# Cross-attention in blocks of three score units, keys and values made by halves of 16 heads, on one Trainium2 core

## The chip, the cores and the metric

The kernel runs on one core of a Trainium2 chip. The metric is the device time of one execution in microseconds (us); the time of before is the median of three runs. The engines are TensorE (PE in the rows; PEld is its weight load), VectorE (DVE), ScalarE (ACT), GpSimd (POOL) and SyncE (SP), whose queue here issues nearly every DMA.

## What is computed

A decoder layer on x of shape 4 x 512 x 512 with a context of 4 x 1601 x 512: a gated recurrence (HGRN), a cross-attention, a self-attention and a mixture of experts, each with a post layer norm. The change touches the cross-attention alone:

```python
q = x @ Wq.T                       # 4 x 512 x 512, 32 heads of 16
k_raw = context @ Wk.T             # 4 x 1601 x 512
v_raw = context @ Wv.T
# heads of 16 columns; keys and values stand interleaved in kv
q = _rmsnorm(q); k = _rmsnorm(k)
scores = jnp.einsum('bhnd,bhmd->bhnm', q, k) * 16 ** (-0.5)
attn = jax.nn.softmax(scores, axis=-1)
out = jnp.einsum('bhnm,bhmd->bhnd', attn, v)
```

## The kernel before, in words

Everything is float32. Products of inputs and weights are made in three terms (high x high, high x low, low x high) of fp32r parts by `product3`; it is L120 of the profile.

**Units of work.** The context of a batch is 13 tiles of 128 rows (CT, the last partly filled). A *quad* is 4 heads (HG); a batch has 8 quads (NQ). A *tile* of the softmax is one quad with one context tile: 4 batches x 8 quads x 13 = 416 tiles. A tile has two *score units*, each two matmuls of 64 rows side by side into two PSUM banks (`scores`, L859), and for each unit ScalarE makes one exponential of 128x1024 (L705). After both, four matmuls, which run as eight, sum the products with the values into one bank, `o_bank` (L876, the *sum* of the tile). Scores turn through three pairs of banks, the probabilities through two buffers.

**Pieces.** What feeds the softmax is cut into pieces. X transposes a tile of x (L830) and VectorE splits it (L738, L740). Q, K and V are projections of 12 matmuls each, in two halves of 6. K and V use all 512 columns, 32 heads. VectorE copies the results (L744 `raw`, L755 `vt`), makes the mean squares (L713 to L719), GpSimd the power of -1/2 (L683 `c_rr`), and VectorE scales (L725 `c_kn`). T transposes the scaled keys or queries (L843) and VectorE splits them (L770, L772). SP stores keys, queries and values into the DRAM tensors `kd`, `qd`, `vd` (L598, L611, L602) and loads them as quads `kq`, `qq`, `vq` (L635, L622, L626), double-buffered. O transposes the sums of a finished quad (L847), and VectorE adds them to X (L778 to L784). All pieces of the softmax share one PSUM bank, bank 7.

**Order.** `Timeline` writes the order out. A prologue makes all pieces of batch 0 (4 X, 4 Q, 13 K, 13 V, 17 T), stores them, and then both of its first quads are loaded. Then comes one loop over the 416 tiles, where TensorE has for each tile: two score units ahead, the sum of the tile, then at most one piece or half product, `line.after[lt]`. The pieces of batch b+1 lie under the softmax of batch b, so the softmax of batch 3 has O pieces alone. In the prologue ScalarE makes the high parts of the context tiles (L699) and VectorE the low ones (L731); later GpSimd makes both (L671, L673), behind its power for the job.

The inner part of TensorE's loop before:

```python
for u in (2 * lt + 3, 2 * lt + 4):
    if u < UNITS:
        scores(u)
pe.wait_ge(s_ex, 2 * lt + 2)
...
for piece in line.after[lt]:
    put(piece)
```

Of the kernel before, what the change touches and what calls it, by code (L numbers as in the profile page):

```python
# [19 lines left out]
P = 128  # L20
# [11 lines left out]
HG = 4  # L32
# [426 lines left out]
class Piece:  # L459


    def __init__(self, kind, job, half, last, item):
        self.kind, self.job, self.half, self.last, self.item = kind, job, half, last, item


class Timeline:


    JOBS = TT + CT
    LTS = (XH // HG) * CT  # L470

    def __init__(self):
        self.items, self.index = 0, {}
        self.prologue = [p for p in self.steps(0)]
        self.prologue_items = self.items
        total = B * self.LTS
        self.after = [[] for _ in range(total + 4)]
        for b in range(B):
            todo = self.plan(b + 1) if b + 1 < B else []
            for lt in range(b * self.LTS, (b + 1) * self.LTS):  # L480
                if lt > CT and lt % CT == 1:
                    self.after[lt] = [self.piece("O", lt // CT - 1, 0, 1)]
                elif todo:
                    kind, job, half, halves = todo[0]
                    if half + 1 == halves and lt % CT == CT - 1:
                        continue
                    self.after[lt] = [self.piece(*todo.pop(0))]
            assert not todo
        self.after[total + 1] = [self.piece("O", total // CT - 1, 0, 1)]

    def plan(self, b):
        at = lambda j: b * self.JOBS + j
        turn = lambda j: [("T", at(j), 0, 1)]
        project = lambda kind, j: [(kind, at(j), 0, 2), (kind, at(j), 1, 2)]
        out = [("X", at(0), 0, 1)]
        for j in range(TT):
            if j + 1 < TT:
                out.append(("X", at(j + 1), 0, 1))
            out += project("Q", j)
            if j >= 2:  # L500
                out += turn(j - 2)
        for j in range(TT, self.JOBS):
            out += project("K", j) + turn(j - 2) + project("V", j)
        return out + turn(self.JOBS - 2) + turn(self.JOBS - 1)

    def steps(self, b):
        return [self.piece(*s) for s in self.plan(b)]
# [8 lines left out]
def cross_attention(nc, X, ident, d):  # L516
# [16 lines left out]
    with ExitStack() as stack:  # L533
# [51 lines left out]
        def _(sp):  # L585
# [27 lines left out]
            def load_quad(q):  # L613
                b, g = divmod(q, NQ)
                if q >= 2:
                    sp.wait_ge(s_pv, (q - 1) * CT)
# [1554 lines left out]
```

## Time and profile before

| | us |
|---|---|
| median of 3 runs | 2739.5 |
| lowest and highest run | 2735.27, 2741.12 |
| the profiled execution's own time | 2738.39 |
| its span | 2736.5 |
| PE, ACT, DVE, POOL busy in the span | 2487.8, 1380.7, 1317.9, 806.4 |

Busy time of an engine is a union over its instructions. Matmuls overlap in the rows: the start of one to the start of the next is what a matmul takes of the engine's time, and its own duration is longer. Times in the rows are us from the span's start. The cross-attention stands between about 224 and 1459.

### The profile page before, as it was taken

The numbers are of one execution on the slowest core, as the hardware profiler recorded it, in microseconds if no ns is written. First come the engines' busy times: TensorE is split into PE (matmuls) and PEld (weight loads), VectorE is DVE, ScalarE is ACT, GpSimd is POOL, SyncE is SP. The second block draws the span as 40 slices with busy tenths as digits, with TensorE's granted clock in tenths as the row PEclk, the third lists the DMA queues.
The fourth block names the chain that finished last, engine by engine and source line by source line (L and its number), as shares of the span: only waits on it lengthen the run. The fifth ranks groups of instructions, "written<-read, shape, count | busy, mean of one in ns | idle before, by whom it ended". The sixth has DMA issues, their size and how long they took to land. (4 is left out here: it accounts for less than half of the span.)

```text
span 2736.5 us, 38571 instructions
## 1 busy us (share of the span) xinstructions
PE 2487.8 (91%) x15376; PEld 1535.7 (56%) x15376; DVE 1317.9 (48%) x1994; ACT 1380.7 (50%) x1695; POOL 806.4 (29%) x485
## 2 busy tenths in 40 slices
PE   7996869999999999999995999998589999999997
PEld 5874734443444334442223555564368788888776
DVE  5565733333433343331004555555365576666675
ACT  4221137667666776669994433433222255555221
POOL 1224735441544244430003333331022021111220
PEclk9997989999999999999997999999799999999999
DMA  4002655546275535555534200000343266665331
GB/s 169 16 1 73 200 132 139 160 121 161 67 196 142 137 81 168 137 130 130 118 79 162 86 1 5 13 17 1 122 146 131 85 206 216 236 212 183 112 124 54
DMA packets 216578, 319.35 MB, mean 117 GB/s; under 512 B 68880, under 2 KB 134416, under 8 KB 216208
## 3 DMA queue, kind: packets, MB, share of 16 engines
q1 hardware_dynamic: 201344, 248.85, 31.4%
q0 software_dynamic: 15056, 68.03, 7.4%
q8 instruction: 123, 2.02, 0.3%
q14 instruction: 55, 0.45, 0.1%
HBM read 229.47 MB, written 99.42 MB: 120 GB/s over the span
## 5 line engine op out<-in xcount | busy, mean ns | idle before, releaser
L705 ACT ACTIVATE c_prob<-c_psum 128x1024 f32<-128x1024 f32 x832 | 815.1, 1036 | 292.0 <-PE c_psum L859 212.8
L683 POOL TENSOR_TENSOR c_rr<-c_ms,c_half 128x32 f32<-128x32 f32 x68 | 372.9, 5485 | 396.0 <-DVE c_ms L719 396.0
L876 PE MATMUL c_psum<-c_prob,c_vq 128*17 128x512 f32 x3328 | 439.2, 599 | 5.2 <-DVE c_oT L803 4.2
L859 PE MATMUL c_psum<-c_qq,c_kq 64*128 64x512 f32 x1664 | 329.8, 462 | 19.2 <-DMA c_kq<-kd 18.3
L859 PEld LDWEIGHTS c_psum<-c_qq,c_kq 64*128 64x128 f32 x1664 | 134.5, 186 | 249.0 <-ACT c_prob L705 206.6
L120 PE MATMUL c_psum<-c_w_hi,c_c_hi 128*128 128x512 f32 x416 | 183.2, 440 | 0.2 <-DVE c_t_lo L772 0.2
L1219 DVE TENSOR_REDUCE s_topx<-s_psum 128x4 f32<-128x2048 f32 (+1 forms) x64 | 95.5, 1493 | 181.7 <-PE s_psum L1309 181.7
L120 PE MATMUL m_psum<-m_t_hi,m_up_hi 128*128 128x256 f32 (+1 forms) x552 | 159.4, 289 | 23.9 <-DVE m_t_lo L1969 23.9
L1742 ACT ACTIVATE m_a_hi<-m_work 128x256 fp32r<-128x256 f32 (+2 forms) x113 | 56.7, 501 | 245.9 <-DVE m_work L1818 241.7
L744 DVE COPY c_raw<-c_psum 128x512 f32<-128x512 f32 x68 | 47.0, 691 | 263.6 <-PE c_psum L120 253.9
L120 PE MATMUL c_psum<-c_w_hi,c_c_lo 128*128 128x512 f32 x416 | 165.5, 398 | 0.0
L120 PE MATMUL c_psum<-c_w_lo,c_c_hi 128*128 128x512 f32 x416 | 165.0, 397 | 0.0
L120 PEld LDWEIGHTS c_psum<-c_w_hi,c_c_hi 128*128 128x128 f32 x416 | 78.6, 189 | 144.6 <-issue 66.3
L120 PE MATMUL m_psum<-m_t_lo,m_up_hi 128*128 128x256 f32 (+1 forms) x552 | 155.2, 281 | 0.0
L120 PE MATMUL m_psum<-m_t_hi,m_up_lo 128*128 128x256 f32 (+1 forms) x552 | 155.0, 281 | 0.0
L1146 ACT ACTIVATE s_pT<-s_psum 128x2048 f32<-128x2048 f32 (+1 forms) x64 | 79.5, 1241 | 129.5 <-PE s_psum L1323 129.2
L120 PE MATMUL m_psum<-m_h_hi,m_up_hi 128*128 128x512 f32 x352 | 139.8, 397 | 2.8 <-DVE m_work L1818 2.8
L120 PE MATMUL m_psum<-m_h_hi,m_up_lo 128*128 128x512 f32 x352 | 139.4, 396 | 0.0
L120 PE MATMUL m_psum<-m_h_lo,m_up_hi 128*128 128x512 f32 x352 | 138.9, 394 | 0.0
L876 PEld LDWEIGHTS c_psum<-c_prob,c_vq 128*17 128x17 f32 x3328 | 55.7, 95 | 145.2 <-issue 111.1
L2043 PE MATMUL m_psum<-m_dn_hi,m_a_hi 128*128 128x512 f32 (+1 forms) x314 | 125.4, 399 | 11.4 <-DVE m_a_lo L1823 11.4
L755 DVE COPY c_vt<-c_psum 128x512 f32<-128x512 f32 x52 | 35.9, 690 | 189.8 <-PE c_psum L120 189.8
(278 smaller groups left out, 4872.2 us busy)
## 6 DMA issues: line engine op xcount, KB each, us to landing
c_kq<-kd SPq DMA_DIRECT2D x256, 208.0 KB
c_qq<-qd SPq DMA_DIRECT2D x64, 256.0 KB
vd<-c_vt SPq DMA_DIRECT2D x52, 272.0 KB, 3.7
c_vq<-vd SPq DMA_DIRECT2D x32, 442.0 KB
c_c_raw<-in_ctxT SPq DMA_DIRECT2D x52, 256.0 KB, 4.1
kd<-c_t_hi SPq DMA_DIRECT2D x52, 256.0 KB, 2.3
kd<-c_t_lo SPq DMA_DIRECT2D x52, 256.0 KB, 3.1
m_hs<-slots SPq DMA_DIRECT2D x23, 512.0 KB, 7.4
```

The source lines that it names most:

```text
L120: mm = pe.matmul(out, a(c), b(c), start=first and i == 0, stop=last and i == len(terms) - 1)
L683: pool.tensor_tensor(rr[:, job % 2, :], ms[:, job % 2, :], half[:], ALU.pow).then_inc(s_r, 1)
L705: act.activation(prob[:, lt % 2, 2 * (u % 2):2 * (u % 2) + 2, :], score_banks[u % 3], ACT.Exp, scale=XD ** -0.5).then_inc(s_ex, 1)
L744: dve.tensor_copy(raw[:, job % 2], src[:]).then_inc(s_got, 1)
L755: dve.tensor_copy(vt[:, v_buf(n), :, 0:XD], heads(src[:])).then_inc(s_got, 1)
L859: mm = pe.matmul(score_banks[u % 3][:, s, :], kq[rows, q % 2, u % 2, lt % CT * P:(lt % CT + 1) * P], qq[rows, q % 2, u % 2, :], start=True ...
L876: mm = pe.matmul(o_bank[32 * j:32 * j + VW, :], vq[:, q % 2, kt, j, :], prob[:, lt % 2, j, :], start=kt == 0, stop=kt == CT - 1)
L1146: act.activation(pT[:, kt % 2, :, 0:L], psum[:, 0:HPC, 0:L], ACT.Exp, scale=SCALE).then_inc(s_ex, 1)
L1219: dve.reduce_max(topx[:, t, ::SD], psum[:, 0:HPC, 0:(t + 1) * P], AX_X).then_inc(s_top, 1)
L1742: act.activation(a_hi[0:rows, p % 2, i, 0:width], act_f[0:rows, 0:width], ACT.Copy).then_inc(s_ahi, 1)
L2043: mm = pe.matmul(y_bank[t], a[0:rows, p % 2, i, ts], w[0:rows, i, :], start=k == 0, stop=k == 3 * len(x.chunks) - 1)
```

## The change

The cross-attention's order, its buffers and its projections are rewritten; the other stages stay.

- **Halves of 16 heads.** A context tile is now projected once for each half of the heads: one product of 12 matmuls gives 256 columns of keys and 256 of values (piece KV). 8 halves x 13 tiles = 104 KV pieces in place of 52 K and 52 V. The columns of the weights are laid out for this outside the kernel. Each context tile is loaded and split twice.
- **Units of the norm.** A unit is one tile of queries or two context tiles of 16 heads; mean square, power, scaling (in place in `raw`, which has 4 buffers now) and transposes are done by unit: 72 in all, where 68 were.
- **The prologue** makes the queries and the first half of batch 0 alone: 4 X, 4 Q, 13 KV, 8 T. ScalarE copies keys and values out of PSUM there, VectorE did before. The weights of keys and values are loaded and split in two halves.
- **The first quad** is loaded in three pieces, context tiles 0 to 5, 6 to 9 and 10 to 12, each as soon as its keys are stored; the transposes of tiles 8 to 12 stand in the softmax's first three blocks.
- **Blocks.** The softmax is 278 blocks of three score units (two more blocks have no scores). In each: three score units, the sums of the tiles whose two units lie in earlier blocks (one and two in turn), then at most one piece, and a product is one whole piece of 12 matmuls. Ten times a piece stands between the two sums, where the second begins a quad. Probabilities have 3 buffers.
- **The planner.** `softmax()` spreads the pieces by due times. Over the blocks stand 103 products (91 KV, 12 Q), 64 T, 32 O and 12 X; 69 blocks have none. Of the products 92 are in blocks with one sum and 11 in blocks with two; of the T, O and X 88 are in blocks with two sums and 20 in blocks with fewer. The second half of batch 3 is made in the softmax of its first half, so the product-free stretch at the end is some 40 blocks.
- GpSimd does one power for two KV pieces, but two operations of splitting for each.

TensorE, early in the softmax of batch 0, **before**: two score units, one sum, half a product, and again.

```order
L859 MATMUL c_psum<-c_qq,c_kq 128x512 x4
L876 MATMUL c_psum<-c_prob,c_vq 17x512 x4
L120 MATMUL c_psum<-c_wq_hi,c_c_hi 128x512
L120 MATMUL c_psum<-c_wq_lo,c_c_hi 128x512
L120 MATMUL c_psum<-c_wq_hi,c_c_lo 128x512
L120 MATMUL c_psum<-c_wq_hi,c_c_hi 128x512
L120 MATMUL c_psum<-c_wq_lo,c_c_hi 128x512
L120 MATMUL c_psum<-c_wq_hi,c_c_lo 128x512
L859 MATMUL c_psum<-c_qq,c_kq 128x512 x4
L876 MATMUL c_psum<-c_prob,c_vq 17x512 x4
L830 MATMUL c_psum<-ident,X 128x128 x4
```

TensorE at a like place **of the changed kernel** (L1057 is the scores, L1066 the sum, L1038 a transpose of keys):

```order
L1057 MATMUL c_psum<-c_qq,c_kq 128x512 x6
L1066 MATMUL c_psum<-c_prob,c_vq 17x512 x8
L1038 MATMUL c_psum<-ident,c_raw 128x128 x4
L1057 MATMUL c_psum<-c_qq,c_kq 128x512 x6
L1066 MATMUL c_psum<-c_prob,c_vq 17x512 x4
L120 MATMUL c_psum<-c_w_hi,c_c_hi 128x512
L120 MATMUL c_psum<-c_w_lo,c_c_hi 128x512
L120 MATMUL c_psum<-c_w_hi,c_c_lo 128x512
```

Nine more rows of L120 follow before the next scores: the six score matmuls and the two sums stand together, and the product is not cut.

GpSimd in the softmax, **before**: a power, then the split of one context tile.

```order
L683 TENSOR_TENSOR c_rr<-c_ms,c_half 128x32
L671 CAST c_c_hi<-c_c_raw 128x512
L673 TENSOR_TENSOR c_c_lo<-c_c_raw,c_c_hi 128x512
L683 TENSOR_TENSOR c_rr<-c_ms,c_half 128x32
L671 CAST c_c_hi<-c_c_raw 128x512
```

GpSimd **of the changed kernel**, in its first half of the softmax:

```order
L809 TENSOR_TENSOR c_rr<-c_ms,c_half 128x32
L800 CAST c_c_hi<-c_c_raw 128x512
L802 TENSOR_TENSOR c_c_lo<-c_c_raw,c_c_hi 128x512
L800 CAST c_c_hi<-c_c_raw 128x512
L802 TENSOR_TENSOR c_c_lo<-c_c_raw,c_c_hi 128x512
L809 TENSOR_TENSOR c_rr<-c_ms,c_half 128x32
```

The power now stands ahead of the first of two splits, and the product two places on waits for that split.

SP's queue **of the changed kernel** at the first quad's first piece (L712 stores values, L697 loads context, L705 stores keys, L740 to L754 load the quad):

```order
L712 DMA vd<-c_vt 128x272
L697 DMA c_c_raw<-in_ctxT 128x512
L705 DMA kd<-c_t_hi 128x2x256
L705 DMA kd<-c_t_lo 128x2x256
L740 DMA c_qq<-qd 128x512 x2
L749 DMA c_kq<-kd 32x768 x8
L754 DMA c_vq<-vd 128x6x68
L712 DMA vd<-c_vt 128x272
```

Before, the quad's loads stood behind every store of the batch; now they stand behind the stores of ten values tiles, of the queries and of six tiles of keys.

The diff, cut to its core:

```diff
+    QT, KU = TT, -(-CT // 2)
+    UPB = QT + 2 * KU
+    FIRST = (0, 6, 10, CT)
+    def first_half(self):
+        return [x(0), x(1), q(0), x(2), q(1), x(3), q(2), q(3), kv(0), t(0), kv(1), t(1), kv(2), t(2), kv(3), t(3), kv(4), kv(5), t(4),
+                kv(6), kv(7), t(5), kv(8), kv(9), t(6), kv(10), kv(11), t(7), kv(12)]
...
+            ready = [t for t in range(done, self.TILES) if 2 * t + 1 <= 3 * k - 1] if k else []
...
+                return placed(self.kind_of(self.job_of(kind, i) - 2), 2)
...
+            if t_ready and turns[0] < line_up:
+                got = ("T", turns.pop(0))
+            elif heavy_ready() and (len(ready) < 2 or k >= due[heavy[0]] + 3):
+                got = heavy.pop(0)
...
+            for piece in line.prologue:
+                store(piece)
+                first_quad(piece)
...
+            for piece in line.items:
+                if piece.kind in ("Q", "KV"):
+                    if line.ends(piece.kind, piece.i):
+                        root(line.unit_of(piece.kind, piece.i))
+                    job = line.job_of(piece.kind, piece.i) + 2
+                    if job < B * line.JPB and line.kind_of(job)[0] == "KV" and line.kind_of(job)[1] >= CT:
+                        split(job)
...
+                        s = i // CT % 2
+                        pe.wait_ge(s_wlo, 2 + s)
+                        pe.wait_ge(s_clo, i + 1)
+                        rhs = (lambda c: w_hi[:, c, s * H:(s + 1) * H], lambda c: w_lo[:, c, s * H:(s + 1) * H])
+                    mm = product3(pe, dst[:], *lhs, *rhs, KC)
...
             for piece in line.prologue:
                 put(piece)
-            pe.wait_ge(s_got, line.prologue_items)
-            for u in range(3):
-                scores(u)
-            for lt in range(B * LTS):
-                q, kt = divmod(lt, CT)
-                for u in (2 * lt + 3, 2 * lt + 4):
-                    if u < UNITS:
-                        scores(u)
+            for piece in line.prologue[-8:]:
+                emptied(piece)
+            for k in range(BLOCKS):
+                for u in range(3 * k, min(3 * k + 3, UNITS)):
+                    scores(u)
+                for t in line.sums[k][0:1 if line.split_pair[k] else 2]:
+                    weighted(t)
+                if line.fill[k]:
+                    put(line.fill[k])
+                if line.split_pair[k]:
+                    weighted(line.sums[k][1])
```

## Rows read from the trace of the kernel before

**Rows 1.** Windows: length, busy PE, PEld, DVE, ACT, POOL; PEclk, DMA share, GB/s

```profile
376.30:671.40 295.10, 291.30 (x1734) 122.44 (x1736) 98.23 (x169) 210.34 (x211) 121.97 (x43) 0.99 0.50 133
...
1257.40:1446.80 189.40, 188.76 (x1260) 54.03 (x1262) 18.65 (x44) 187.85 (x205) 1.01 (x1) 1.00 0.43 100
```

**Rows 2.** Windows of the prologue, same columns

```profile
279.00:311.00 32.00, 27.81 (x128) 22.06 (x127) 23.25 (x40) 3.05 (x5) 24.64 (x6) 1.00 0.70 220
...
360.00:376.00 16.00, 0.00 (x0) 0.00 (x0) 0.00 (x0) 0.00 (x0) 0.00 (x0) 0.50 1.00 236
```

**Rows 3.** Waits of TensorE from 223 to 380: us in total, times, longest

```profile
PE c_psum L859 <- DMA c_kq<-kd: 18.3, 1, 18.3
PE c_psum L843 <- DVE c_kn L725: 16.1, 7, 3.3
PE c_psum L120 <- DVE c_c_lo L740: 14.3, 2, 9.2
```

**Rows 4.** Timeline of the prologue: start us, us, engine, line, operation, idle before

```profile
249.19 4.41 DVE L797 TENSOR_TENSOR c_w_lo<-c_w_raw,c_w_hi 128x4096 fp32r<-128x4096 f32 x1
...
255.08 0.76 PE L120 MATMUL c_psum<-c_wq_hi,c_c_hi 128*128 128x512 f32 x1 [5.09 <-DVE c_c_lo L740]
...
259.63 0.48 PE L120 MATMUL c_psum<-c_w_hi,c_c_hi 128*128 128x512 f32 x1
...
376.34 1.65 PE L859 MATMUL c_psum<-c_qq,c_kq 64*128 64x512 f32 x6 [18.25 <-DMA c_kq<-kd]
...
382.77 1.22 PE L859 MATMUL c_psum<-c_qq,c_kq 64*128 64x512 f32 x4
```

**Rows 5.** Timeline of TensorE, one tile with half a product, one with a T

```profile
540.30 0.73 PE L859 MATMUL c_psum<-c_qq,c_kq 64*128 64x512 f32 x4
540.96 1.05 PE L876 MATMUL c_psum<-c_prob,c_vq 128*17 128x512 f32 x8
541.95 0.51 PE L120 MATMUL c_psum<-c_w_hi,c_c_hi 128*128 128x512 f32 x1
542.29 0.40 PE L120 MATMUL c_psum<-c_w_lo,c_c_hi 128*128 128x512 f32 x1
542.52 0.40 PE L120 MATMUL c_psum<-c_w_hi,c_c_lo 128*128 128x512 f32 x1
...
543.54 0.73 PE L859 MATMUL c_psum<-c_qq,c_kq 64*128 64x512 f32 x4
...
551.68 0.66 PE L843 MATMUL c_psum<-ident,c_kn 128*128 128x128 f32 x4
552.27 0.73 PE L859 MATMUL c_psum<-c_qq,c_kq 64*128 64x512 f32 x4
```

**Rows 6.** Product-free end: group (busy, mean ns, idle before), then ScalarE's exponentials in a window

```profile
L859 PEld LDWEIGHTS c_psum<-c_qq,c_kq 64*128 64x128 f32 x344 | 31.2, 183 | 85.3 <-ACT c_prob L705 81.7 <-issue 1.9
...
1265.00:1425.00 160.00, 158.86 (x173) 1.00 0.46 107
```

**Rows 7.** Timeline of SP's queue: stores of the prologue, loads of the first quad

```profile
290.73 1.21 SPq L602 DMA_DIRECT2D vd<-c_vt  x1
...
299.92 1.17 SPq L602 DMA_DIRECT2D vd<-c_vt  x1
...
360.58 1.16 SPq L622 DMA_DIRECT2D c_qq<-qd  x2
...
363.07 3.75 SPq L635 DMA_DIRECT2D c_kq<-kd  x8
```

**Rows 8.** GpSimd's power and split: durations ns least, median, most

```profile
L683 POOL TENSOR_TENSOR c_rr<-c_ms,c_half x68: 5421/5430/5806, 243.1 to 1219.5; 128x32 f32<-128x32 f32 x68
...
L673 POOL TENSOR_TENSOR c_c_lo<-c_c_raw,c_c_hi x39: 1282/1646/1652, 419.1 to 1193.9; 128x512 fp32r<-128x512 f32 x39
...
L671 POOL CAST c_c_hi<-c_c_raw x39: 604/611/613, 418.4 to 1193.2; 128x512 fp32r<-128x512 f32 x39
```

**Rows 9.** Groups by line from 223 to 376: busy us, mean ns, idle before

```profile
L713 DVE TENSOR_TENSOR c_sq<-c_raw 128x512 f32<-128x512 f32 x17 | 11.8, 692 | 0.5
```

More of the change, by code:

```diff
@@ L459, with __init__ @@
 class Piece:
-    def __init__(self, kind, job, half, last, item):
-        self.kind, self.job, self.half, self.last, self.item = kind, job, half, last, item
+    def __init__(self, kind, i, index, nth):
+        self.kind, self.i, self.index, self.nth = kind, i, index, nth
+        self.normalise = []
 class Timeline:
-    JOBS = TT + CT
-    LTS = (XH // HG) * CT
-    def __init__(self):
[L473 to L504, printed above, removed]
@@ new lines, in store, with load_quad @@
+            def store(piece):
+                if piece.kind == "T" and line.parts(piece.i)[0] == "K":
+                    store_keys(piece)
+                if piece.kind == "KV":
+                    h, lt = divmod(piece.i, CT)
+                    store_values(piece)
+                    if piece.i + CB < 2 * B * CT:
+                        load_ctx(piece.i + CB)
+                    if h % 2 == 0 and 4 <= lt < 4 + KC:
+                        store_queries(h // 2, lt - 4)
+            def load_quad(q, first, last, s_done):
@@ L631, in load_quad @@
+                for i in range(2):
+                    units = [u for u in range(h * KU + -(-last // 2)) if u % 2 == i]
+                    sp.wait_ge(s_kst[i], 32 * len(units))
+                for i, x in pairs:
                     for s in range(2):
-                        rows = kd[b, c, (h + s) * XD:(h + s + 1) * XD].rearrange("e r n -> (e r) n")
+                        rows = kd[b, c, (x + s) * XD:(x + s + 1) * XD, :, first * P:last * P].rearrange("e r n -> (e r) n")
                         for a in range(2):
@@ L736, in take @@
+            def take(piece, early, units):
+                i, src = piece.i, bank_of(piece)
+                if piece.kind != "KV" or not early:
+                    dve.wait_ge(s_put, piece.index + 1)
                 if piece.kind == "X":
+                    job = line.job_of("Q", i)
                     chunks = src[:].rearrange("p (k t) -> p k t", k=KC)
+                    if job >= 2:
+                        dve.wait_ge(s_put, line.of[line.kind_of(job - 2)].index + 1)
                     own.done(dve.tensor_copy(c_hi[:, job % 2], chunks))
@@ L759, in take @@
+                if piece.kind == "KV" and early and i + 2 < CT:
+                    split_low(i + 2)
                 if piece.kind == "T":
-                    b, j = divmod(job, JOBS)
-                    if is_q(job):
+                    what = line.parts(i)
+                    if what[0] == "Q":
+                        b, j = divmod(what[1], TT)
                         if b and j == 0:
@@ L817, in _, with emptied @@
         def _(pe):
[L818 to L826 removed]
+            def emptied(piece):
+                if piece.kind == "KV":
+                    pe.wait_ge(s_k, piece.nth)
+                    pe.wait_ge(s_v, piece.nth)
+                else:
+                    pe.wait_ge({"X": s_x, "Q": s_q, "T": s_t, "O": s_o}[piece.kind], piece.nth)
```

548 lines of the change are left out of this document (344 added, 204 removed).

## The prediction

> **What bounds the kernel now.** I read the windows by stage first, then the waits and the timeline of TensorE at the two places that the change rewrites, then the queues that feed them. The windows show two regimes in the softmax. Under the pieces of the next batch TensorE is busy 291.3 of 295.1 us and ScalarE 210.3; in the last batch both are full, TensorE 188.8 and ScalarE 187.9 of 189.4 [rows 1]. A full TensorE may still be waiting, so the weight loads decide: in the product-free end the score weights stand idle 81.7 of 160 us for ScalarE [rows 6]. There ScalarE sets the pace, 173 exponentials in 160 us, 0.925 each or 1.85 us per tile [rows 6]. In the other regime TensorE's own work does: a tile with half a product takes 543.54 - 540.30 = 3.245 us without a gap, one with a T 2.235 [rows 5]. Before the softmax lies a prologue that is nobody's full load: TensorE waits there 18.3 us for the first quad, 16.1 for scaled keys and 14.3 for split inputs [rows 3], and no exponential runs until 376.3 [rows 4].
>
> The switches matter. Within a product the matmuls are 0.234 us apart, but the first of one takes 0.34, and two score units take 0.66, so about 0.1 is lost at the start and at the end of each kind of matmul; a sum takes 0.985 [rows 5].
>
> **The prologue after.** The first product of keys began at 259.6 [rows 4]. VectorE's split of the weights (4.41 us) stood before the last input's split, and TensorE waited 5.1 us for that [rows 4]; half the weights come there now, so I put the first KV at 255. TensorE then has 13 products of 2.8 us (12 x 0.234) and 8 groups of transposes of 0.59 [rows 5]: 41 us, to 296. GpSimd made its first power at 243.1; eight at 5.43 end by 287 [rows 8], in time for T7.
>
> SP's queue is slower than that. With the queries among the stores it issued without a break, and one tile's round (values, context, four of queries, two of keys, 2.1 MB) took 299.92 - 290.73 = 9.2 us [rows 7]; the window gives 220 GB/s [rows 2]. The same queries are now stored with KV4 to KV7, from about 271. Until the keys of tiles 4 and 5 are out, the queue has six value stores of 136 KB, six contexts of 256, sixteen of queries and six of keys at 256: 8.2 MB, 37 us at 220 GB/s, so 308. The first piece of the quad follows: 1.5 MB, 7 us at the same rate, no more than the 3.75 us of its eight issues [rows 7] and a landing. First scores at **315** in place of 376.3: **-61 us**. If transfers did not limit, TensorE's 296 and the load would give 306 (-70); if each of four tiles with queries costs the old round of 9.2 us and the load takes the 15.8 us from 360.58 to 376.3 [rows 4, 7], it is 326 (-50). The transposes of the tiles 8 to 12 are inside the softmax, where a block takes over 2.8 us; tile 6 is scored in block 4, some 13 us in, and its transposes, stores and 4-tile load need about as much. I take 0 and keep 5 us in the range.
>
> **The softmax before, as a check.** 180 half products at 3.245, 95 T, O and X at 2.235 and 141 bare tiles at 1.85: 584 + 212 + 261 = 1057. From 376.3 to the last sum, at 1448.6, the trace has 1072. The other 15 us are the slow start and waits early in a batch, and I carry them over.
>
> **The softmax after, by blocks.** Two score units take 0.66. The third is bounded by 0.34 (a first one) from above; its nearest row is the start of the softmax, where the clock had fallen to 0.50 in the wait [rows 2] and three units last 1.65 where two last 1.22 [rows 4]: 0.43 at half the clock, 0.215 at the full one. I take that: 0.88 for three. One sum is 0.98. Two sums in a row have no row: 1.86 if the 0.1 of a switch is saved, as inside a product, 1.96 if not; I take 1.86. A product in one piece: 1.59 + 6 x 0.234 = 2.99. Then
> - 92 blocks with a product and one sum: 0.88 + 0.98 + 2.99 = 4.85, 446 us;
> - 11 with a product and two sums: 5.73, 63 us;
> - 88 with T, O or X and two sums: 0.88 + 1.86 + 0.59 = 3.33, 293 us;
> - 20 with T, O or X and fewer sums, and 69 with nothing: TensorE has 1.9 to 2.75 us of work, less than three exponentials, 3 x 0.925 = 2.775 [rows 6]: 89 x 2.775 = 247, less 2 us for the two at the ends.
>
> Sum 1047. ScalarE's 2.775 per block fits into every block with a product, and into 3.33. So alternating blocks are TensorE's, and only the bare ones ScalarE's. With the 15 us carried over: 1062.
>
> Here a rule can be weighed. The rows show 0.1 us at each change of the matmul's shape [rows 5]. The Trainium skill, TensorEngine Tiling (Array Packing), Key Properties, says that changing the tiling mode drains the engine; by it the longer runs save what I assume, and the trace agrees as far as it goes. Without the saving (0.34 for the middle unit, 1.96 for two sums) the 191 blocks that TensorE sets get 0.13 us each and 99 of them 0.1 more: +35 us.
>
> **The waits that the order adds.** A product waits for the low part of its context tile, which GpSimd makes two products ahead, behind a power if that product ended a unit. The chain from such a product: four VectorE operations of about 0.69 [rows 9], 2.8, then 5.43, 0.61 and 1.65 [rows 8], 10.5 us. Between products in alternate blocks lie 3.33 + 4.85 + 3.33 + 1.86 = 13.4 us: hidden. Where three products follow each other, or keys follow the last query, only 7.6 us lie between, and TensorE stands 3 us; six such places count with half to all of that: +12 us. VectorE's operations for 512 columns are the same as before: nothing. Context loads double, 52 more of 256 KB or 13 MB over 1070 us, 12 GB/s beside 133 [rows 1], half of the DMA time being free: nothing. A half's first quad is loaded at least four blocks ahead, one of them (heads 16 to 31 of batch 0) with only some 11 us for stores and a load that need 15: 4 us, which I count as part of the 15 carried over. Result 1074, against 1072: **+2 us**, bounds -25 (nothing carried over, no chain waits) and +37.
>
> **Sum.** 2738.4 - 61 + 2 = 2679 for the profiled execution, which is 1.1 us under the median of 2739.5; the tail after the last sum and the other stages are untouched. The ends together would be 2738.4 - 70 - 25 = 2643 and 2738.4 - 50 + 37 = 2725; all of one sign at once is unlikely, and the third rival's time is inside: **2650 to 2718**.
>
> **Rivals.**
> - *A leaner loop* (0.2). The carried waits came from pieces that now have other places, and a third prob buffer lets ScalarE run ahead. Speaks for it: without products a block is 2.30 us of TensorE's work on average where 1.5 old tiles were 2.46, and a product 2.99 where it was 3.18. Against: 103 products must still find their low parts. Softmax 1047 to 1055, time about 2656.
> - *No saving at the switches* (0.12): +35 us on TensorE's blocks, about 2714.
> - *The first quad comes late* (0.12). SP's queue is in order, so the piece stands behind all query stores, and the small loads and stores together go slower than 220 GB/s; then the second piece and quad 1 queue as well. First scores at 330 and 6 us lost after: 2738 - 46 + 8 = 2700.
> - *GpSimd's chain sets the pace* (0.05), and the kernel is slower. Each pair of products costs one power and two splits in series behind VectorE. For each us by which the chain is over the 13.4 us that are there, some 45 pairs pay 45 us. At 14.7 us, 4.2 over my count, the 59 us are gone; at 16 it is 2679 + 117 = 2796. Against it: the power never took over 5.81 us, and the split between 1.28 and 1.65 [rows 8], so it would need VectorE to be late by a whole block each time. The Trainium skill, GPSIMD Engine Reference, Key points, says that GpSimd shares its SBUF interfaces with VectorE and contends with operations of two SBUF inputs. The spread of 0.37 us in the split may be that.
> - That the loop starts no earlier, because something holds it that the old order hid, I give 0.01: no change.
>
> The forecast itself has 0.5. A measurement of this kernel tells some 0.2 % (5 us) from no change. All but the last two are faster: faster 0.94, within 0.2 % 0.01, slower 0.05.
>
> **What would show it.** The first exponential near 315 and TensorE's wait before it under 20 us. SP issuing without gaps from about 271 to 308. A product block of 4.85 us, a transpose block with two sums of 3.3, inner score step 0.21 to 0.23. TensorE waits for c_c_lo at c. six places of 2 to 3 us and hardly elsewhere. From the first scores to the last sum about 1074. Wrong if that is over 1105, if GpSimd waits are common in alternate blocks, or if the first scores are after 326.

## The result, and the profile after

The changed kernel takes **2720.43 us** (median of 3 runs, 2717.23 to 2721.36) against 2739.5: ratio 0.9931, 95 % interval 0.9908 to 0.9953. It is faster, but by 19 us where 60 were forecast, and outside the range. Its profiled span is 2718.7 us where 2736.5 was; of the 17.8 us, the cross-attention gives 20.2 (its last sum starts at 1428.39, before at 1448.58) and 2.4 are lost after it.

| | before | forecast | after |
|---|---|---|---|
| first scores | 376.34 | 315 | 324.28 |
| first scores to the start of the last sum | 1072.2 | 1074 | 1104.1 |
| sum of both | 1448.6 | 1389 | 1428.4 |

So the prologue gives 9 us less than forecast, and the softmax takes 30 us more.

Windows of the changed kernel; the first two answer to [rows 1], the third to the first of [rows 2], the last is one product behind a wait. Columns as there.

```profile
324.30:628.80 304.50, 281.88 (x1726) 136.20 (x1726) 110.44 (x216) 194.13 (x205) 156.78 (x78) 0.97 0.60 158
1230.00:1427.00 197.00, 182.87 (x1238) 66.65 (x1234) 35.56 (x69) 172.79 (x185) 35.03 (x17) 1.00 0.43 104
279.00:311.00 32.00, 21.40 (x84) 16.30 (x84) 13.96 (x24) 5.41 (x15) 17.55 (x4) 0.89 0.65 200
...
496.30:499.60 3.30, 3.30 (x10) 2.53 (x9) 0.00 (x0) 0.00 (x0) 1.16 (x1) 0.50 0.00 0
```

TensorE was busy 98.7 % of its first stretch before and is busy 92.6 % now, and its mean clock there fell from 0.99 to 0.97. That is the first sign that the softmax has waits which it did not have.

**The blocks cost what was forecast.** From the timeline of TensorE I took the time from a block's first score matmul to the next block's. The medians:

| kind of block | count | forecast | median |
|---|---|---|---|
| a whole product, one sum | 92 | 4.85 | 4.88 |
| a product, two sums in a row | 9 | 5.73 | 5.73 |
| T, O or X, two sums in a row | 84 | 3.33 | 3.32 |
| nothing (mean) | 67 | 2.775 | 2.80 |

With the few other forms and every block at the median of its kind (the bare ones at their sum) this is 1041.5 us, where the forecast has 1047. (Other ways to group the rare forms give 1038 to 1046.) One block as the timeline of TensorE has it, and what answers to [rows 5]:

```profile
491.41 0.97 PE L1057 MATMUL c_psum<-c_qq,c_kq 64*128 64x512 f32 x6
492.30 1.05 PE L1066 MATMUL c_psum<-c_prob,c_vq 128*17 128x512 f32 x8
495.69 0.47 PE L120 MATMUL c_psum<-c_w_hi,c_c_hi 128*128 128x512 f32 x1 [2.34 <-POOL c_c_lo L802]
...
496.60 0.63 PE L120 MATMUL c_psum<-c_w_hi,c_c_hi 128*128 128x512 f32 x1
497.02 0.63 PE L120 MATMUL c_psum<-c_w_lo,c_c_hi 128*128 128x512 f32 x1
...
500.19 0.97 PE L1057 MATMUL c_psum<-c_qq,c_kq 64*128 64x512 f32 x6
501.09 1.91 PE L1066 MATMUL c_psum<-c_prob,c_vq 128*17 128x512 f32 x16
502.93 0.66 PE L1042 MATMUL c_psum<-ident,c_oT 128*128 128x128 f32 x4
503.52 0.74 PE L1057 MATMUL c_psum<-c_qq,c_kq 64*128 64x512 f32 x4
```

Three units 0.89, one sum 0.98, two 1.84, a T or O 0.59: the prices used. But this is also one of the late blocks: 8.79 us from 491.41 to 500.19. It stands 2.34 us for the low part of its context tile, and the product behind the wait takes 4.5 us where 3.0 was counted. Its first matmuls are at full speed; then they stand 0.43 apart in place of 0.234, which the window from 496.3 shows as a granted clock of 0.50 (1.2 GHz, where it had been 2.4 before the wait). This wait of 2.3 us costs **3.9**. Four of the five waits for GpSimd do. The fifth, 2.28 us at 395.08, costs its own length alone: the product behind it takes 2.97 us.

**What lies over the medians.** The last block with scores leads to the last two sums, which start at 1427.20. From the first scores to there are 1102.9 us, and the variants below are measured to the same place. 1102.9 - 1041.5 = 61 us, where the forecast had 27 (15 carried over, 12 for GpSimd). Of it 46 are in fourteen blocks: 12.5 at quad 6, 6.7 at quad 1, 20.6 at the five waits for GpSimd with what follows them, 4.8 in three transpose blocks that come after bare ones, 1.2 in one other. The waits of TensorE from 324 to 1440 (us, times, longest):

```profile
PE c_psum L1057 <- ACT c_prob L861: 17.7, 54, 0.5
PE c_psum L1057 <- DMA c_vq<-vd: 15.6, 3, 9.8
PE c_psum L120 <- POOL c_c_lo L802: 11.5, 5, 2.3
...
PE c_psum L1038 <- DVE c_raw L884: 3.1, 5, 0.7
```

The first row is ScalarE's pace in bare blocks and is in the medians. **Quad 6** is the 9.8 us. In SP's queue (L740, L749, L754 are its load):

```profile
523.24 0.43 SPq L697 DMA_DIRECT2D c_c_raw<-in_ctxT  x1
532.71 1.21 SPq L718 DMA_DIRECT2D qd<-c_q_hi  x2
...
543.88 2.86 SPq L740 DMA_DIRECT2D c_qq<-qd  x2
546.84 4.05 SPq L749 DMA_DIRECT2D c_kq<-kd  x8
551.00 0.38 SPq L754 DMA_DIRECT2D c_vq<-vd  x1
```

The load stands in SP's order behind the pieces of the blocks that start at 516.6 and 523.0. But both of these carry stores of the next batch's queries, which wait for the last transpose of these queries, and that stands in the block of 527.8. From 523.7 to 532.7 SP issues nothing, and the DMA share is 0.16; then 8 query stores go first, and the quad lands at 562.

**The prologue.** The first product of keys begins at 256.9 (255 forecast), the first query store at 278.94 (271). SP's queue then:

```profile
278.94 1.40 SPq L718 DMA_DIRECT2D qd<-c_q_hi  x2
280.39 2.04 SPq L718 DMA_DIRECT2D qd<-c_q_lo  x2
282.48 1.27 SPq L712 DMA_DIRECT2D vd<-c_vt  x1
283.79 1.86 SPq L697 DMA_DIRECT2D c_c_raw<-in_ctxT  x1
...
313.65 0.46 SPq L705 DMA_DIRECT2D kd<-c_t_lo  x1
314.22 1.16 SPq L740 DMA_DIRECT2D c_qq<-qd  x2
```

Why the first query store is late, in two rows of VectorE (L893 is half of the weights' low part, L940 the end of the last queries' split):

```profile
275.31 2.29 DVE L893 TENSOR_TENSOR c_w_lo<-c_w_raw,c_w_hi 128x2048 fp32r<-128x2048 f32 x1
...
278.23 0.69 DVE L940 TENSOR_TENSOR c_q_lo<-c_psum,c_q_hi 128x512 fp32r<-128x512 f32 x1
```

And ScalarE's waits from 280 to 322, then TensorE's from 223 to 330, which answer to [rows 3]:

```profile
ACT c_c_hi L838 <- DMA c_c_raw<-in_ctxT: 26.6, 4, 8.7
ACT c_c_hi L838 <- PE c_psum L120: 4.1, 1, 4.1
```

```profile
PE c_psum L1038 <- DVE c_raw L884: 15.2, 3, 7.5
...
PE c_psum L1057 <- DMA c_vq<-vd: 1.4, 1, 1.4
```

From the first query store to the load of the quad the queue runs without a gap, as forecast, and takes 35.3 us (37 forecast). But it begins 8 us late: the first keys 1.9 late, TensorE's wait of 1.8 at 268.97, and then the second half of the weights, which VectorE splits ahead of the last queries; their split ends at 278.92. The load takes 10.1 us to the first scores where 7 was counted. With 1.7 us less for the queue that is the 9.3.

The other thing that was not forecast: the context loads stand between the query stores, so ScalarE waits 26.6 us for context tiles, VectorE behind it, and TensorE 15.2 us for scaled keys; its last product ends at 322.9, not 296. From 300 to 320 its clock is 0.67. TensorE still waits 1.36 us for the load, so the load, and not TensorE, came last.

### The profile page after: what moved, and what is told of

Its sections match the earlier page's. It is cut to its first block and busy times, and to the rows that moved or that the text cites. A ratio compares the mean times of both kernels' runs of the same rounds, so it can differ in the third digit from the quotient of the medians.

```text
span 2718.7 us, 38977 instructions
## 1 busy us (share of the span) xinstructions
PE 2443.4 (90%) x15376; PEld 1565.7 (58%) x15376; DVE 1338.2 (49%) x2097; ACT 1358.8 (50%) x1722; POOL 901.9 (33%) x593
## 5 line engine op out<-in xcount | busy, mean ns | idle before, releaser
L861 ACT ACTIVATE c_prob<-c_psum 128x1024 f32<-128x1024 f32 x832 | 786.3, 1031 | 317.1 <-PE c_psum L1057 308.6
L809 POOL TENSOR_TENSOR c_rr<-c_ms,c_half 128x32 f32<-128x32 f32 (+1 forms) x72 | 372.8, 5179 | 450.0 <-DVE c_ms L878 449.9
L1066 PE MATMUL c_psum<-c_prob,c_vq 128*17 128x512 f32 x3328 | 416.4, 600 | 6.1 <-DVE c_oT L981 6.0
L1057 PE MATMUL c_psum<-c_qq,c_kq 64*128 64x512 f32 x1664 | 292.4, 439 | 35.6 <-ACT c_prob L861 17.7
L1057 PEld LDWEIGHTS c_psum<-c_qq,c_kq 64*128 64x128 f32 x1664 | 137.4, 185 | 196.4 <-ACT c_prob L861 109.7
L918 DVE COPY c_raw<-c_psum 128x256 f32<-128x256 f32 x91 | 38.7, 425 | 364.8 <-PE c_psum L120 364.8
L120 PE MATMUL c_psum<-c_w_hi,c_c_hi 128*128 128x512 f32 x416 | 179.0, 430 | 15.1 <-POOL c_c_lo L802 11.5
L120 PE MATMUL m_psum<-m_t_hi,m_up_hi 128*128 128x256 f32 (+1 forms) x552 | 159.4, 289 | 23.9 <-DVE m_t_lo L2168 23.9
L1066 PEld LDWEIGHTS c_psum<-c_prob,c_vq 128*17 128x17 f32 x3328 | 68.7, 96 | 185.2 <-issue 160.9
L120 PE MATMUL c_psum<-c_w_hi,c_c_lo 128*128 128x512 f32 x416 | 168.8, 406 | 0.0
L120 PE MATMUL c_psum<-c_w_lo,c_c_hi 128*128 128x512 f32 x416 | 167.8, 403 | 0.0
L120 PE MATMUL m_psum<-m_t_lo,m_up_hi 128*128 128x256 f32 (+1 forms) x552 | 155.1, 281 | 0.0
L120 PE MATMUL m_psum<-m_t_hi,m_up_lo 128*128 128x256 f32 (+1 forms) x552 | 155.0, 281 | 0.0
L120 PEld LDWEIGHTS c_psum<-c_w_hi,c_c_hi 128*128 128x128 f32 x416 | 80.7, 194 | 108.7 <-issue 58.6
L120 PE MATMUL m_psum<-m_h_hi,m_up_hi 128*128 128x512 f32 x352 | 139.8, 397 | 2.8 <-DVE m_work L2017 2.8
L120 PE MATMUL m_psum<-m_h_hi,m_up_lo 128*128 128x512 f32 x352 | 139.4, 396 | 0.0
L120 PE MATMUL m_psum<-m_h_lo,m_up_hi 128*128 128x512 f32 x352 | 138.9, 395 | 0.0
L1848 POOL DMA_INDIRECT m_up_raw<-in_up,m_up_row x46 | 43.5, 947 | 276.9 <-DVE m_up_lo L1979 276.9
```

Source lines behind the costliest of these rows:

```text
L120: mm = pe.matmul(out, a(c), b(c), start=first and i == 0, stop=last and i == len(terms) - 1)
L809: pool.tensor_tensor(rr[:, unit % RB, 0:n], ms[:, unit % RB, 0:n], half[:, 0:n], ALU.pow).then_inc(s_r, 1)
L861: act.activation(prob[:, t % PB, 2 * (u % 2):2 * (u % 2) + 2, :], score_banks[u % 3], ACT.Exp, scale=XD ** -0.5).then_inc(s_ex, 1)
L918: dve.tensor_copy(raw[:, unit % RB, at:at + HD], src[:, 0:HD]).then_inc(s_k, 1)
L1057: mm = pe.matmul(score_banks[u % 3][:, s, :], kq[rows, q % 2, u % 2, kt * P:(kt + 1) * P], qq[rows, q % 2, u % 2, :], start=True, stop=True)
L1066: mm = pe.matmul(o_bank[32 * j:32 * j + VW, :], vq[:, q % 2, kt, j, :], prob[:, t % PB, j, :], start=kt == 0, stop=kt == CT - 1)
```

## The experiments

Two theories. (The expectations call a transpose a turning.) **A**: SP's in-order queue, and above all the query stores in it, makes the first scores, quad 1 and quad 6 late. **B**: GpSimd's chain (the power ahead of the split) costs four or five places 3.9 us each. The rival to both: TensorE itself or the block's form takes the time. Where two kernels were not run together they are compared by their ratio to the kernel before; by it the changed kernel's 0.9931 stands for 2720. Each kernel is the changed one with the edit shown.

### GpSimd's order (split_first)

```diff
+ ends, early = line.ends(piece.kind, piece.i), piece.index < len(line.prologue)
- if line.ends(piece.kind, piece.i):
+ if ends and early:
      root(line.unit_of(piece.kind, piece.i))
...
      split(job)
+ if ends and not early:
+     root(line.unit_of(piece.kind, piece.i))
```

> GpSimd copies and subtracts the next-but-one context tile before it takes the power, instead of after. Theory B (the power and the copies in one row on GpSimd set the five waits of 2.3 us in places where three products follow one another): the five waits for the low half of a context tile (11.5 us in all) and the half-speed stretch of the product behind each (some 1.6 us a place) go, 2720 falls by 15 to 19 us, to about 2703. Theory A (SP's queue alone costs the time, GpSimd's place is covered by other waits): 2720 stays within 4 us. It may also lengthen the way to a turning of keys, by 4.2 us, which the trace would show as waits of TensorE for the normalised keys.

2717.93 us, ratio 0.9924 (0.991 to 0.9937): 2.5 us by the medians, 2 by the ratios, not 15 to 19, and no more than the intervals leave open. The waits for `c_c_lo` are gone. But at two places, where the product's block took 8.7 us and the next one 4.7, the product's now takes 5.3 and 4.9 and the next one 9.1 and 9.0: its transpose waits. In the timeline of the first place (L887 makes what the transpose needs):

```profile
840.79 0.61 POOL L800 CAST c_c_hi<-c_c_raw 128x512 fp32r<-128x512 f32 x1
...
846.70 0.43 DVE L924 COPY c_vt<-c_psum 128x256 f32<-128x256 f32 x1 [2.82 <-DMA vd<-c_vt]
847.04 0.68 DVE L887 TENSOR_TENSOR c_raw<-c_raw,c_rr 128x512 f32<-128x512 f32 x1
```

GpSimd's power had ended at 840.8. VectorE's scaling stood behind a copy of values, and that waited for the store of an older value tile in SP's queue. At the second place VectorE's copy waits 6.90 us for the same. So at these two places A's resource takes 8.7 us of the some 18 that the five products give back. (The expectation of shift_split below names the context tile and a late power for this; the rows say that it was the value store.)

### Query stores later (q_shift)

```diff
- if h % 2 == 0 and 4 <= lt < 4 + KC:
-     store_queries(h // 2, lt - 4)
+ at = 6 if h else 4
+ if h % 2 == 0 and at <= lt < at + KC:
+     store_queries(h // 2, lt - at)
```

> The stores of the queries of batches 1 to 3 stand behind the 7th to 10th product of their batch instead of the 5th to 8th. Theory A (quad 6's load stands in SP's queue behind a query store that waits for a turning two blocks on): the wait of 9.8 us at 562 and the 2.7 us in the block behind it go, 2720 falls by 10 to 12 us. Theory B, or that the load is late for its bytes and not for its place in the queue: the wait stays above 6 us and the time within 4 us of 2720.

2703.27 us, ratio 0.9874 (0.9857 to 0.9891): 17 us faster by the medians, 16 by the ratios. Quad 6's load now goes at 525.23, ahead of the stores, and its scores start on time at 548.10. In SP's queue:

```profile
524.75 0.43 SPq L697 DMA_DIRECT2D c_c_raw<-in_ctxT  x1
525.23 0.93 SPq L741 DMA_DIRECT2D c_qq<-qd  x2
...
535.56 2.29 SPq L718 DMA_DIRECT2D qd<-c_q_hi  x2
```

It was the place in the queue: the same bytes are moved. In its loop the time from first scores to last sums is 1088.5, 14.4 less. That is not quad 6's 12.5 alone. The stores now stand ahead of quad 7's load, whose block (581.65) takes 3.8 us over its median with a wait of 2.16. On the other side quad 1's wait, which the edit doesn't touch, is 1.66 in this execution where it was 4.46, and its block is 4.8 shorter. The five waits for GpSimd stand as before (11.5 us), but only three of them are followed by a slow product.

### Batch 0's queries later (q_late)

```diff
+ if h == 0 and lt == 4:
+     store_queries(0, 0)
+ if h == 1 and 1 <= lt < KC:
+     store_queries(0, lt)
- if h % 2 == 0 and 4 <= lt < 4 + KC:
+ if h and h % 2 == 0 and 4 <= lt < 4 + KC:
      store_queries(h // 2, lt - 4)
...
- if g == 0 and first == 0:
+ if b == 0 and g == 0 and first == 0:
+     sp.wait_ge(s_qst, 16 * 4)
+ elif (g == 0 and first == 0) or (b == 0 and g >= 2):
      sp.wait_ge(s_qst, 16 * 4 * KC * (b + 1))
```

> Of batch 0's queries only chunk 0 is stored ahead of the first quad (0.5 MB instead of 2.1 MB of the packed layout's writes), chunks 1 to 3 behind the 15th to 17th key and value product, in the softmax. Theory A (the query stores, issued from 279 to 314 us between the context loads, set the first scores): the waits for a context tile in the stretch 289 to 318 shrink from some 4 to 9 us each to under 2, first scores at 305 to 312 instead of 324.3, the wait for quad 1 (4.5 us) goes or shrinks, the time falls by 12 to 20 us. Rival (the products and the turnings themselves, or DVE and ScalarE, set the first scores): first scores stay within 3 us of 324 and the time within 4 us.

2709.2 us, ratio 0.9899 (0.9884 to 0.9915), 9 to 11 us faster, where 12 to 20 were expected. (By the sizes in the trace the stores ahead of the first quad are 1.0 MB in place of 4.2, not 0.5 in place of 2.1.) The first scores come at 307.42, 17 us earlier, where A put them, and ScalarE's waits for context tiles fall from 26.6 to 6.7 us. The 3.1 MB that moved away are 14 us at 220 GB/s, so this run doesn't tell what the stores cost by their bytes from what they cost by holding up context tiles. The load of the first quad in SP's queue, and a row of VectorE:

```profile
298.43 0.91 SPq L746 DMA_DIRECT2D c_qq<-qd  x2
300.62 3.58 SPq L755 DMA_DIRECT2D c_kq<-kd  x8
304.31 0.38 SPq L760 DMA_DIRECT2D c_vq<-vd  x1
...
381.18 0.42 DVE L927 COPY c_vt<-c_psum 128x256 f32<-128x256 f32 x1 [5.12 <-DMA vd<-c_vt]
```

6 us of it are given back in the softmax, 3.5 of them in the block at 375.5: by the order, quad 2's load waits for all query stores (SP stands from 362.0 to 367.7), value stores queue behind it, and VectorE's copy of values waits for those (the last row). The wait for quad 1 did not shrink. A transfer that is moved out of one stage is not gone.

### All three (all3), and two of them (shift_split)

The diffs are those above together; the second is without the edit of batch 0's queries.

> The three edits together. If the two theories speak of separate places the gains add up: 2720 less 16 (GpSimd's order), less 11 (quad 6), less 16 (first scores and quad 1), about 2677, between 2670 and 2690. If one of them only moves a wait elsewhere, it stays above 2695.

> Query stores later and GpSimd's order changed, both, without the edit of batch 0's queries. With GpSimd's order changed alone the time fell by 0.5 us only: its five waits were gone, but TensorE then stood 5.8 and 5.7 us in two other blocks, where GpSimd's copy waited for a context tile that SP had issued behind query stores, and the power behind the copy came late. Theory C (the two are one chain: GpSimd's gain is eaten by SP's queue): with the context tiles no longer behind those stores the two new waits go, and the order is worth 12 to 16 us on top of the 15 us of the later stores: 2687 to 2692. Rival (GpSimd's order is worth nothing by itself, since the power is then late in every such place): within 4 us of 2703.

All three: 2687.96, ratio 0.9815 (0.9802 to 0.9828), inside the forecast and at its upper end. The three single gains against 2720.4 are 2.5, 17.2 and 11.2, together 31, where 16, 11 and 16 were expected; all at once are 32. Two: 2698.63, ratio 0.9867 (0.9852 to 0.9882). By the medians GpSimd's order is worth 4.6 us on top of the later stores, by the ratios 2, and the intervals overlap; its runs spread over 10 us. The theory's 12 to 16 fall, the rival's nothing does not. The profiled executions give 5.2 in the softmax, while TensorE's waits for `c_vq` from 330 us on are 6.8 us in one and 3.8 in the other. The waits at the products, 11.5 us and some 5 of slow work behind them, are gone; more than half of that is spent elsewhere. By the order, the power now stands behind a copy and a split, some 1.9 us, on its way to every transpose; that this is where the rest went was not tested by itself.

### A longer chain on GpSimd (pow_8)

```diff
+ if unit >= 12:
+     pool.wait_ge(s_idle, unit - 12)
+     pool.tensor_tensor(idle[:, 0:8], ms[:, unit % RB, 0:8], half[:, 0:8], ALU.pow).then_inc(s_idle, 1)
  pool.tensor_tensor(rr[:, unit % RB, 0:n], ...
```

> One more power of 8 columns, some 1.4 us, before each power on GpSimd from the 13th unit on; the values are not used. The chain from a product to the low part of the next-but-one tile grows from 10.5 to some 11.9 us, against 13.4 us between products in alternate blocks. If that account of slack is right, only the five places that wait already pay, 1.4 us each: 7 us more, 2724 to 2730. If the chain is already at its limit in alternate blocks, some 45 pairs of products pay 1.4 us each: 63 us more, about 2780.

2752.8 us, ratio 1.0062 (1.0048 to 1.0076): 32 us more, between the two. The added power takes 1.64. Waits of TensorE from 330 to 1461:

```profile
PE c_psum L120 <- POOL c_c_lo L804: 25.4, 10, 3.9
...
PE c_psum L1043 <- DVE c_raw L889: 12.1, 13, 2.3
...
PE c_psum L1038 <- DVE c_raw L889: 4.6, 4, 1.9
```

The waits for the low part go from 5 to 10, none at every alternate block: that part of the slack account holds roughly. But 17 transposes now wait 16.7 us for scaled keys or queries, where 6 waited 3.4. The forecast had counted the chain only to the next split. The one to the transpose is closer to its limit. The softmax takes 35.2 us more, of which these waits are 27.

### The first quad in one piece (one_piece)

```diff
- FIRST = (0, 6, 10, CT)
+ FIRST = (0, CT)
- kv(11), t(7), kv(12)]
+ kv(11), t(7), kv(12), t(8), t(9), t(10)]
```

> The first quad is loaded whole, behind the keys of all 13 tiles, whose last three turnings stand in the prologue again. First scores at some 344 us instead of 324 (the last power, the turning, its stores and a whole load follow the last product, which ends at 323), and the 7 us that TensorE loses for quad 1 at 358 go: 12 to 15 us more, about 2733. If the load in three pieces brings nothing, because SP's queue is the limit in any case, the time stays within 4 us of 2720.

2732.99 us, ratio 0.9981 (0.9971 to 0.999), as expected. The edit also puts quad 1's load right behind the whole quad 0. First scores at 346.90 behind a wait of 16.77 for the load; the softmax then takes 1093.9, 9 less than with three pieces. Quad 1 is there (6.7 us), and one wait for GpSimd is gone (2.3). The other four stand, 2.27 to 2.34 us each, but none is followed by a slow product here, which is 6 us; other blocks take some of that back. The window of the product behind the first of them:

```profile
509.50:513.00 3.50, 3.50 (x18) 2.55 (x18) 0.51 (x2) 0.08 (x1) 1.63 (x2) 1.00 0.00 0
```

So the pieces give 22.6 us at the start and lose up to 9 of them, and a part of the 9 is not theirs. The same wait costs 2.3 in one kernel and 3.9 in another: of the 18 waits of 2.27 to 2.34 us in the traces of the changed kernel, q_shift, q_late and this one, eleven have a product of 4.4 to 4.5 us behind them and seven one of 3.0. What decides was not tested.

### Blocks of two units (two_units, two_gap)

```diff
- blocks = -(-self.UNITS // 3)
+ blocks = -(-self.UNITS // 2)
- edge = lambda h: 104 * h / 3
+ edge = lambda h: 52 * h
- ... if 2 * t + 1 <= 3 * k - 1]
+ ... if 2 * t + 1 <= 2 * k - 1]
- for u in range(3 * k, min(3 * k + 3, UNITS)):
+ for u in range(2 * k, min(2 * k + 2, UNITS)):
```

The second has also `unit_done[...] <= k - 5` for the 3 of the planner's rule for transposes.

> Blocks of two score units (one tile) and one sum instead of three and one or two; all else as in the changed kernel, the product stays whole. By the rows: 103 blocks with a product at 0.66 + 0.98 + 2.99 = 4.63, 108 with T, O or X at 2.23, 205 bare at 1.85: 1097 us against 1042 for blocks of three, 55 us more. Against that stand the waits, which should be rarer, since two blocks lie between products almost everywhere: up to 40 us less. So 2735 to 2775. If the form of the block is worth nothing (the rival that switches between matmul shapes cost nothing) it is 2680 to 2720.

2845.09 us, ratio 1.0398 (1.0382 to 1.0414): far over the range.

```profile
PE c_psum L1038 <- DVE c_raw L884: 80.5, 39, 7.1
```

39 transposes wait for scaled keys. The planner's gap of three is in blocks, and a block is shorter now. The expectation had looked at the products alone.

> Blocks of two units again, with the turning of keys five blocks behind its product instead of three. The run before (2845) gave 1097 us for the blocks' own time, as the rows said, and some 130 us of waits for scaled keys with slow stretches behind them, since three of the shorter blocks don't cover GpSimd's power. With five blocks that goes: 1100 to 1125 us from the first scores to the last sum, against 1104 in the changed kernel with its waits: 2720 to 2740. That would say that blocks of three are worth some 55 us in TensorE's own time, and that the changed kernel gives up to 40 us of it back in waits. If it stays above 2780, the shorter blocks cost something that this account lacks.

2735.72 us, ratio 0.9985 (0.9975 to 0.9994). From first scores to last sum:

```profile
324.80:1443.60 1118.80, 1072.09 (x6624) 448.68 (x6624) 380.27 (x755) 783.67 (x832) 502.43 (x247) 0.99 0.56 143
```

The time is inside the expectation. From first scores to last sums are 1118.8 us, with no wait for a low part. TensorE's busy time is 1072.1 against 1046.3 from 324.3 to 1428.6 in the changed kernel, for the same matmuls (but for twelve at the ends). With every block at the median of its kind it is 1096, the 55 us more than 1041.5 that the rows had given, and 23 lie over that, 9.5 of them at one early transpose that waits 6.7 us for scaled keys and the block behind it. So blocks of three save 55 us in the blocks' own time, and the changed kernel gives 38 of them back by its 61 us of lateness against 23.

### The planner's gaps, stores spread out, quad 1 in pieces (gap, stores_spread, best)

```diff
- return placed(self.kind_of(self.job_of(kind, i) - 2), 2)
+ return placed(self.kind_of(self.job_of(kind, i) - 2), 3)
- t_ready = ... and unit_done[turns[0]] <= k - 3
+ beside = any(p and p.kind in ("Q", "KV") for p in fill[-2:])
+ t_ready = ... <= k - (3 if beside or unit_done[turns[0]] < 0 else 4)
...
+ self_at = lambda b, c: (4, CT + 1, CT + 6, CT + 10)[c] if b == 0 else 2 * b * CT + 6 + 3 * c
- if h % 2 == 0 and 4 <= lt < 4 + KC:
-     store_queries(h // 2, lt - 4)
+ for c in range(KC):
+     if piece.i == self_at(h // 2, c):
+         store_queries(h // 2, c)
...
+ load_quad(1, 0, line.FIRST[1], s_second[0])
- load_quad(1, 0, CT, s_quad[1])
+ load_quad(1, line.FIRST[1], CT, s_second[1])
```

The first part is `gap` (with the edit of q_shift), the second is added in `stores_spread`, the third in `best`.

> As the run with query stores later (2703), with two changes of the planner: a product never stands less than three blocks behind the product two before it, whose power GpSimd may have in hand, and a turning of keys stands four blocks behind its product where both blocks between are bare. If time for GpSimd's chain is what those places lack, and not its order, the four waits of 2.3 us with their half-speed product behind (3.9 us each, 15 us) and the turnings' waits in three places (1.5 us each) go with nothing in exchange: 2703 less 15 to 20, 2683 to 2688, below the run that changed GpSimd's order instead (2699). If waits only move elsewhere again: 2695 to 2703.

2693.44 us, ratio 0.9843 (0.9829 to 0.9856): 10 less than q_shift, not 15 to 20. No wait for a low part is left in the softmax, and GpSimd's order was not touched. But the planner's rule also moved the last keys of the second half two blocks later, and quad 4 waits:

```profile
PE c_psum L1059 <- DMA c_vq<-vd: 9.7, 4, 5.7
```

5.7 us of wait make that block 7.6 longer; without it the gain would be some 17, by this estimate.

> The planner's two changes, and one semaphore per chunk of queries: chunk 0 of batch 0 is stored in the prologue, chunks 1 to 3 behind the 15th, 20th and 24th product, those of later batches from the 7th on, three products apart; a quad waits for its own chunk only. First scores at 307 as in the run with batch 0's queries late, without that run's wait for quad 2 (its load stood for all query stores, and blocks 15's 5.8 us came of it). 2685 less 15 to 17: 2668 to 2672; the wait for quad 1 (4 to 5 us) stays.

> The run before with quad 1 loaded in two pieces as well, the first of them at the end of the prologue, where SP's queue stood empty for some 4 us. The wait for quad 1 goes: 4 to 6 us less, 2664 to 2668. If its 1.2 MB delay the second and third piece of quad 0, first scores or the tiles 6 and 10 are late instead and nothing is gained.

2682.28 us, ratio 0.98 (0.9787 to 0.9813): 11 less, not 15 to 17. Its first scores are at 308.53; the wait for quad 2 is gone, and a product at 588.0 now waits 3.24 us for VectorE's low parts of keys. And 2681.06, ratio 0.9792 (0.9779 to 0.9805): quad 1 in pieces brings nothing, as the expectation's second half says. The wait for quad 1 went and two others came:

```profile
321.18 0.42 DVE L945 CAST c_t_hi<-c_psum 128x256 fp32r<-128x256 f32 x1 [4.79 <-DMA kd<-c_t_lo]
...
322.12 0.50 PE L120 MATMUL c_psum<-c_w_hi,c_c_hi 128*128 128x512 f32 x1 [2.52 <-DVE c_t_lo L947]
...
327.21 1.65 PE L1066 MATMUL c_psum<-c_qq,c_kq 64*128 64x512 f32 x6 [2.03 <-DMA c_vq<-vd]
```

The key stores queue behind quad 1's piece, VectorE's buffer is not free, and quad 0's second piece is late. The last kernel is the fastest of the set: 57 us less than the kernel before, 38 to 39 less than the changed one. Quad 4 still waits 5.4 us in it.

## Why the prediction was wrong

The measured time lies some 41 us over the forecast: 9 in the prologue, 30 in the softmax, 2 behind it. The two steps that failed are the start of the query stores in the prologue and, above all, the 15 us carried over in the softmax. The forecast's own signs did not catch it: the first scores were to come by 326 and came at 324.28, the softmax was to stay under 1105 and took 1104.1. Each part lay just inside its bound, both at the slow end, which the forecast had called unlikely. By its own steps:

- **Blocks of three: right.** 1041.5 against 1047, each kind within 0.03 us, and blocks of two cost the 55 us more that the same prices give. The rival without a saving at the switches falls. The rule of the Trainium skill, TensorEngine Tiling (Array Packing), Key Properties, is that changing the mode drains the engine. The trace agrees: fewer changes of shape take 1046 us of busy TensorE where more take 1072.
- **"with KV4 to KV7, from about 271" ... "so 308": the step of the prologue that failed**, by 9 us. Bytes and rate were right: 35.3 us against 37, no gap. The start was at 278.94, 8 us late. The step followed TensorE's products there and not VectorE, which had half the weights to split ahead of the last queries. The load took 10.1 us, not 7. The step also took the stores for a load on SP alone; they held up the context tiles too, and TensorE's last product with them, though the load came later still. That the stores are what sets the first scores q_late shows: with three quarters of them out of the way, 307.
- **"With the 15 us carried over" and "which I count as part of the 15 carried over": the step of the softmax that failed**, mis-sized and of the wrong cause: 15 us, where some 40 of the 61 lie outside GpSimd's five places. The waits of the changed kernel are not those of before. 12.5 us at quad 6 came from a store that waits for a transpose ahead of a load that was ready to go; q_shift took it away. I had followed SP's order in the prologue and not in the softmax, though each query store stands in it behind a product and each load at a fixed block. The 5 us kept in the range for the first quad's pieces is less than the 6.7 at quad 1. The 4 us counted for heads 16 to 31 of batch 0 did not come: quad 4 has no wait in the changed kernel. Some 21 us lie in many small waits, for which no run was made.
- **"Six such places count with half to all": the mechanism right, the size low.** Five places waited 11.5 us against 12. The place costs 3.9 in four of them, since most of the product behind runs at 1.2 GHz, and 2.3 in the fifth; 20.6 us in all. The forecast used the loss of clock as a price for score units [rows 2] and never as the price of a wait. The Trainium skill, TensorE: Matmul & The Clock Gate, HAM oscillation, says that a wait for data can throttle the engine for the work behind it. Here it did after a wait of 2.34 us, and did not after one of 2.28; in one_piece it did not after 2.34 either.
- **"GpSimd's chain" as a slower kernel: did not happen**, but pow_8 shows that it was nearer than the forecast's slack of 2.9 us said: the first to run short is the way to the transpose.
- **"First quad late" (2700)** was in kind the nearest rival, with 6 us lost after. 2720 needs late first scores, the query stores at quad 6 and the clock together. The first two come from one queue, while the range had taken unknowns as separate.
- The 2.4 us behind the cross-attention were counted as untouched. No run was made for them. That part takes 1287.9 us before and 1284 to 1291 in the variants' profiled executions, so they stay open.

How far the causes are shown: quad 6 and the first scores each by one edit that only moves query stores. The price of GpSimd's waits is read from the rows and is not fixed; gap shows that they are avoidable, but not fully separated from the wait at quad 4. Quad 1's wait was taken away only in exchange for others, and it varies from 1.7 to 4.5 us between traces whose edits don't touch it.

## What to carry to other kernels

Write an in-order DMA queue out as an engine of its own, beside the compute engines: for each load, every store ahead of it and what that store waits for. Here a load that was ready and stood behind stores that were not cost 12.5 us, while the DMA engines were little used (share 0.16). If the gaps of a planner are in blocks, they must be checked again in us when blocks change. Price a wait of TensorE as a range where matmul work follows: 2.3 us cost 2.3 to 3.9 here.

## What was not expected of the hardware

- A wait of 2.34 us behind a stretch without a gap (TensorE busy all of 480 to 493.3, granted clock 1.00) was followed by a granted clock of 0.50. In one_piece the same wait of 2.34 us behind a like stretch (busy all of 495 to 507, clock 1.00) was followed by 1.00. The wait of 9.77 at quad 6 was followed by 0.50: a block with a transpose and two sums took 5.98 us in place of 3.32.
- GpSimd's power costs by its columns: 5.43 us for 32, 2.90 for 16, 1.64 for 8, so 0.16 a column and 0.4 for itself.
- GpSimd's split took 1.285 us in the median of 90, where it was 1.646 before [rows 8]. Its longest is 1.65 in both.
- SP's issue of two query stores takes 1.2 to 3 us in the crowded stretch, where a store or a load alone takes 0.32 to 0.47 in a quiet one. So in such a stretch the issues themselves take time in SP's queue.
